# A message sum moved from a stage of its own into the mixer and the first feed-forward, and weight splitting moved out of the experts' stage into the mixer

## The chip, the cores and the metric

One NeuronCore of a Trainium2 chip runs the whole program in one launch. The metric is device microseconds of that core, lower is better. Before the change the three runs took 3969.18, 3976.69 and 3976.80 us; the median is 3976.69 us.

## What is computed

Two layers of a graph network on 3125 nodes with 256 channels and 50000 edges sorted by destination. The change touches the first layer alone, whose first half is (cut from the reference):

```python
# graph part, xn = layernorm(x)
h = xn @ W
norm = deg_inv_sqrt[src] * deg_inv_sqrt[dst]
out = segment_sum(h[src] * norm[:, None], dst, num_segments=N)
# mixer part, on the same xn
h = layernorm(x, ln1_g, ln1_b); xm = h @ Wx + bx
q = softmax(xm @ Wq, axis=-1); k = softmax(xm @ Wk, axis=-2); v = xm @ Wv
attn = (q @ (k.T @ v)) @ Wo + bo            # per head
fx = attn + x
m = gelu(layernorm(fx, ln2_g, ln2_b) @ W1 + b1) @ W2 + b2
# joined
x = x + out + (m + fx)
```

Then come eight experts (three 256x256 products each, weighted and added to `x`), and the second layer, whose last stage uses eight more experts with weights `L1_ffn_W1p` and `L1_ffn_W2p`. The graph sum and the mixer both depend only on `xn`, and both are added to `x`.

## The kernel before, in words

Rows lie in SBUF as 25 tiles of 125 nodes (`m.x`, `m.y`, `m.z`); most loops run over 5 chunks of 5 tiles. Products in float32 quality are made of float16 halves: an operand is scaled, its high half is copied by ScalarE and its low half is the rest, computed by VectorE. Each stage is a `phase` with its own tensors, semaphores and a barrier at its end, so stages don't overlap. Every engine runs its own instruction list in order, written by hand, and waits on semaphores.

The stages around the change, in order:

- **`message_sum`** (L646 to L711). The edges are 80 groups of 625. GpSimd issues 5 indirect DMAs per group (L657), each gathering 125 rows of 1 KB from DRAM into one of 4 slots. VectorE copies the indices of a group three ahead (L690), builds a one-hot matrix per group and tile that the group touches (L679), and adds the finished sum into `m.x` (L616, in class `Adder`). TensorE multiplies the one-hot by the gathered rows, 10 matmuls per visit (L708). A group has one visit or two; there are 104 visits. `total` has 4 PSUM banks (`RING`) and the adder runs 2 visits behind (`LAG`).
- **`layernorm_cols`** "ln1", then **`mixer0`** (L933 to L1117). The mixer has a first loop of 5 chunks (L979 to L1000: `mixed`, keys, queries and values), a middle part (softmax of the keys, their product with the values, L1003 to L1099) and a read loop of 5 chunks (L1102 to L1117). GpSimd adds two bias rows to `m.z` and `m.x` (L952).
- **`layernorm`** "ln2", then **`feed_forward`** "ff0": per chunk 16 units of 6 matmuls (L517 by helper `product`), Gelu on ScalarE (L861), two VectorE halves (L886, L888), then 5 row tiles of 24 matmuls (L840) that VectorE adds to `m.x` (L893).
- **`experts0`**: 8 experts times 5 chunks ("steps"). Beside its own work it prepares weights for the last stage: SyncE loads 2 MB of raw weights per expert (L1263, L1266), ScalarE makes the high half of a fifth in each step (L1355), VectorE the low half (L1406), and SyncE stores the halves (L1272). ScalarE and VectorE meet these instructions in order between those of the experts:

```python
act.wait_ge(s_raw, (e + 1) * 32)                                   # ScalarE, end of each step
act.activation(next16[:, 0, piece], next_raw[:, piece], ACT.Copy, scale=WS)
...
dve.wait_ge(s_nhigh, step + 1)                                     # VectorE, after the first row tile
dve.scalar_tensor_tensor(out=next16[:, 1, piece], in0=next_raw[:, piece], ...)
```

Of the kernel before, what the change touches and what calls it, by code (L numbers as in the profile page):

```python
# [15 lines left out]
F32 = mybir.dt.float32  # L16
# [13 lines left out]
J = 5  # L30
# [330 lines left out]
def layernorm(nc, m, name, source, rows_out=None, rows16=None):  # L361

    with phase(nc, name) as ph:
# [19 lines left out]
        with nc.Block() as block:  # L383

# [50 lines left out]
def layernorm_cols(nc, m, name, source, rows_out, cols):  # L435


    with phase(nc, name) as ph:
# [6 lines left out]
        s_normed, s_turned, s_free, s_done, s_rows = (ph.sem(x) for x in ("normed", "turned", "free", "done", "rows"))  # L445
        with nc.Block() as block:

            @block.vector
            def _(dve):
                v = Chain(dve, s_v)  # L450
                with dve.Fori(0, CHUNKS) as c:
                    for j in range(J):
                        ins = dve.bn_stats(stats[:, c * J + j, :], source[:, c * J + j, :])
                    ins.then_inc(s_stats, 1)
# [12 lines left out]
            @block.gpsimd  # L467
            def _(pool):
                if rows_out is not None:
                    with pool.Fori(0, CHUNKS) as c:  # L470
                        for j in range(J):
                            pool.wait_ge(s_normed, c * J + (j + 1))
                            pool.tensor_copy(rows_out[:, c * J + j, :], normed[:, j, :]).then_inc(s_rows, 1)

            @block.scalar
            def _(act):
# [3 lines left out]
                with act.Fori(0, CHUNKS) as c:  # L480
                    for j in range(J):
# [13 lines left out]
                        if rows_out is not None:  # L495
                            act.wait_ge(s_rows, c * J + (j + 1))
# [93 lines left out]
class Adder:  # L590
# [3 lines left out]
    def __init__(self, nc, dve, name, summed, total, s_total, s_added, scale=None):  # L594
        self.scale = scale
        self.nc, self.dve, self.summed, self.total = nc, dve, summed, total
        self.s_total, self.s_added = s_total, s_added
        self.tiles = [dve.alloc_register(f"{name}_tile{n}") for n in range(LAG)]
        for register in self.tiles:
            dve.reg_mov(register, 0)  # L600

    def add(self, visit, tile):
# [4 lines left out]
        fresh = self.total[:, dve.snap((visit + (RING - LAG)) % RING), 0:self.summed.shape[2]]  # L607
        for n in range(LAG - 1):
# [3 lines left out]
        dve.wait_ge(self.s_added, visit + LAG)  # L612
# [6 lines left out]
    def finish(self, visits, s_pace):  # L619

        for n in range(LAG):
            self.add(visits + n, 0)
        self.dve.wait_ge(self.s_added, visits + 2 * LAG)
# [3 lines left out]
def message_sum(nc, m, a):  # L627
# [4 lines left out]


    with phase(nc, "ms") as ph:
        index = ph.sb("index", [R, SLOTS, J], I32)
        got = ph.sb("got", [R, SLOTS, J, 2 * C], F16)
        hot = ph.sb("hot", [R, RING, J, R], F16)
        node = ph.sb("node", [R, T])
        s_node = ph.sem("node")
        total = ph.ps("total", [R, RING, 512])  # L640
        s_index, s_got = ph.sem("index"), [ph.sem(f"got{s}") for s in range(SLOTS)]
        s_hot, s_total, s_added, s_zero = (ph.sem(x) for x in ("hot", "total", "added", "zero"))
        s_pace = ph.sem("pace")
        ph.ahead(*[s_total, s_added] * LAG)

        with nc.Block() as block:  # L646

            @block.gpsimd
            def _(pool):
                pool.iota(node[:, :], pattern=[[R, T]], base=0, channel_multiplier=0,  # L650
                          allow_small_or_imprecise_dtypes=True).then_inc(s_node, 1)
                with pool.Fori(0, G // SLOTS) as i:
                    for s in range(SLOTS):
                        pool.wait_ge(s_index, i * SLOTS + (s + 1))
                        pool.sem_inc(s_pace, 1)
                        for j in range(J):
                            pool.indirect_dma_start(  # L657
                                out=got[:, s, j, :], out_offset=None, in_=m.gather0,
                                in_offset=bass.IndirectOffsetOnAxis(ap=index[:, s, j:j + 1], axis=0)
                            ).then_inc(s_got[s], 16)  # L660

            @block.vector
            def _(dve):
                dve.memset(total[:, :, :], 0.0).then_inc(s_zero, 1)
                dve.wait_ge(s_zero, 1)
                dve.wait_ge(s_node, 1)
                for s in range(SLOTS - 1):
                    dve.tensor_copy(index[:, s, :], m.edge_src[:, s, :]).then_inc(s_index, 1)
                adder = Adder(nc, dve, "ms", m.x, total, s_total, s_added, m.inv_sqrt_degree)

                with dve.Fori(0, G // SLOTS) as i:
                    for s in range(SLOTS):
                        g = i * SLOTS + s
                        first, count, before = group_bounds(dve, m, g)
                        with dve.Fori(0, count) as k:
                            visit = dve.snap(before + k)
                            tile = dve.snap(nc.s_assert_within(first + k, 0, T - 1))

                            dve.scalar_tensor_tensor(out=hot[:, visit % RING, :, :],  # L679
# [2185 lines left out]
```

## Time and profile before

| | us |
|---|---|
| median of three runs | 3976.69 |
| the profiled execution's own time | 3971.04 |
| its span, first to last instruction | 3969.2 |
| TensorE busy | 2597.7 (65%) |
| VectorE busy | 2161.6 (54%) |
| ScalarE busy | 1267.9 (32%) |
| GpSimd busy | 1311.2 (33%) |

The mean granted TensorE clock is 0.797 of full speed. The kernel is a sequence of stages, so a share of the whole span says little; each stage has to be read from its own stretch. "issue" in front of an instruction is time in which its engine waited for nothing that the profile shows, such as reading a register from memory.

### The profile page before, as it was taken

To read this page: it belongs to the slowest core of one execution; us is meant where nothing else is said; L and a number is where in the kernel's file an instruction comes from. 1 tells how busy PE (TensorE), PEld (TensorE's weight loads), DVE (VectorE), ACT (ScalarE), POOL (GpSimd) and SP (SyncE) were. 2 spreads that over 40 slices of the span, in tenths; PEclk is the share of its full clock that TensorE was granted. 3 is DMA by queue.
4 is the path that set the end of the run, shared out by engine and by line. 5 is a ranking of instruction groups with operands and counts; after the bars stand their busy time and mean duration, and the time that the engine had idled before them with its cause. 6 is when DMAs were issued, how large, how long until landed. Compare 5 with 4: busy or idle time off the path is not lost. (4 is left out here: it accounts for less than half of the span.)

```text
span 3969.2 us, 66443 instructions
## 1 busy us (share of the span) xinstructions
PE 2597.7 (65%) x17122; PEld 2094.4 (53%) x17123; DVE 2161.6 (54%) x4413; ACT 1267.9 (32%) x2476; POOL 1311.2 (33%) x1017
## 2 busy tenths in 40 slices
PE   5513333336587698896567777764967543699997
PEld 4413333334267466665455555543855442589986
DVE  6512222231556387787467777765533777644445
ACT  0300000003144154554122222223335774344541
POOL 0048888853000000000188888883000110211115
PEclk9655555557678599997789999996978875699998
DMA  3223333320000112211377777770000000356643
GB/s 110 72 66 84 83 84 83 83 64 6 0 22 0 37 51 100 100 50 71 99 194 189 190 190 191 187 181 28 0 14 0 0 0 0 147 190 237 233 147 90
DMA packets 240037, 364.49 MB, mean 92 GB/s; under 512 B 118099, under 2 KB 173728, under 8 KB 234588
## 3 DMA queue, kind: packets, MB, share of 16 engines
q0 software_dynamic: 154752, 174.53, 17.9%
q1 hardware_dynamic: 72348, 177.00, 12.9%
q10 hardware_dynamic: 12864, 12.06, 1.0%
q8 instruction: 37, 0.61, 0.1%
q14 instruction: 36, 0.29, 0.0%
HBM read 314.79 MB, written 47.76 MB: 91 GB/s over the span
## 5 line engine op out<-in xcount | busy, mean ns | idle before, releaser
L657 POOL DMA_INDIRECT ms_got<-gather,ms_index x400 | 497.6, 1244 | 125.1 <-issue 110.0
L708 PE MATMUL ms_total<-ms_got,ms_hot 125*125 125x256 f16 x1040 | 234.1, 414 | 411.8 <-DMA ms_got<-gather,ms_index 269.5
L1562 POOL DMA_INDIRECT as_gkv<-gather_kv,as_index x340 | 463.7, 1364 | 105.7 <-issue 101.4
L708 PEld LDWEIGHTS ms_total<-ms_got,ms_hot 125*125 x1040 | 205.6, 221 | 440.3 <-issue 440.3
L1554 POOL IOTA as_node<- 125x25 f32 x1 | 0.2, 156 | 1020.7 <-POOLq L116 1020.7
L1679 PE MATMUL as_total<-as_gkv,as_hot 125*125 125x264 f32 x850 | 217.9, 405 | 77.4 <-DVE as_summed L614 70.4
L1342 ACT ACTIVATE ex_h<-ex_up,ex_now 128x313 f32<-128x313 f32 (+1 forms) x320 | 193.7, 612 | 185.6 <-PE ex_up L517 179.7
L1679 PEld LDWEIGHTS as_total<-as_gkv,as_hot 125*125 125x125 f32 x850 | 157.0, 193 | 117.0 <-issue 91.4
L478 ACT ACTIVATE ln_sd<-ln_mv,eps 125x25 f32<-125x25 f32 x1 | 0.3, 317 | 681.0 <-DVEq L73 681.0
L2675 DVE CAST moe_hidden<-moe_h 128x256 f16<-128x256 f32 (+1 forms) x336 | 102.2, 304 | 199.7 <-ACT moe_h L2612 199.6
L2612 ACT ACTIVATE moe_h<-moe_up,wring 128x256 f32<-128x256 f32 (+1 forms) x336 | 163.5, 487 | 128.2 <-PE moe_up L517 85.8
L1654 PE MATMUL as_picked<-y_rows,as_pick 125*125 x1060 | 152.5, 294 | 47.8 <-issue 46.4
L2565 PE MATMUL moe_down<-wring,moe_hidden 128*128 128x256 f16 x1536 | 178.1, 273 | 0.0
L517 PE MATMUL ex_up<-ex_h,ex_w 128*128 128x313 f16 (+1 forms) x960 | 150.6, 318 | 42.0 <-DVE ex_h L1390 42.0
L517 PE MATMUL moe_up<-moe_cols,wring 128*128 128x256 f16 x1536 | 172.9, 273 | 1.4 <-ACT moe_cols L2619 1.4
L1654 PEld LDWEIGHTS as_picked<-y_rows,as_pick 125*125 x1060 | 125.5, 143 | 82.9 <-issue 80.0
L679 DVE SCALAR_TENSOR_TENSOR ms_hot<-row_no,ms_node,edge_dst 125x625 f32 x104 | 90.8, 873 | 134.0 <-issue 134.0
L2453 POOL DMA_INDIRECT moe_rows<-gather,moe_taken x64 | 63.2, 988 | 300.3 <-PE moe_turned L2540 257.7
L1390 DVE TENSOR_TENSOR ex_h<-ex_h 128x313 f16<-128x313 f32 (+1 forms) x320 | 155.4, 486 | 11.0
L517 PEld LDWEIGHTS moe_up<-moe_cols,wring 128*128 128x128 f16 x1536 | 150.2, 98 | 19.0 <-issue 1.6
L616 DVE SCALAR_TENSOR_TENSOR x_rows<-ms_total,inv_sqrt_degree,x_rows x106 | 50.9, 480 | 200.5 <-PE ms_total L708 199.6
L2565 PEld LDWEIGHTS moe_down<-wring,moe_hidden 128*128 128x128 f16 x1536 | 150.4, 98 | 17.3
(454 smaller groups left out, 6045.2 us busy)
## 6 DMA issues: line engine op xcount, KB each, us to landing
wring<-wsplit SPq DMA_DIRECT2D x33, 2052.0 KB
as_dsts<-in_dst SPq DMA_DIRECT2D x83, 305.2 KB
wsplit<-ex_next SPq DMA_DIRECT2D x8, 2048.0 KB, 8.7
ex_next_raw<-in_L_ffn_W1p SPq DMA_DIRECT2D x8, 1024.0 KB, 10.7
ex_next_raw<-in_L_ffn_W2p SPq DMA_DIRECT2D x8, 1024.0 KB, 12.9
results<-moe_made SPq DMA_DIRECT2D x32, 256.0 KB, 7.5
ms_got<-gather,ms_index POOLq DMA_INDIRECT x400
gather_kv<-qkv_out SPq DMA_DIRECT2D x5, 1250.0 KB
```

Of the source, the lines that this page charges most:

```text
L517: ins = pe.matmul(out, left(k, b), right(n, b), start=(i == 0), stop=(i == len(todo) - 1))
L657: pool.indirect_dma_start(out=got[:, s, j, :], out_offset=None, in_=m.gather0, in_offset=bass.IndirectOffsetOnAxis(ap=index[:, s, j:j + 1] ...
L679: dve.scalar_tensor_tensor(out=hot[:, visit % RING, :, :], in0=repeat_mid(m.row_no[0:R, :], J), scalar=node[:, bass.ds(tile, 1)], in1=repe ...
L708: ins = pe.matmul(total[:, visit % RING, 0:C], hot[:, visit % RING, j, :], got[:, s, j, p * C:(p + 1) * C], start=(j + p == 0), stop=(j + ...
L1342: act.activation(h32[:, u % 4, 0:n], up[:, u % 4, 0:n], ACT.Relu, bias=now[:, 1, layer, o:o + 1], scale=now[:, 0, layer, o:o + 1]).then_in ...
L1390: dve.tensor_tensor(to[:, 1, o, at:at + n], full, to[:, 0, o, at:at + n], ALU.subtract).then_inc(s_h, 1)
L1562: pool.indirect_dma_start(out=gkv[s][:, j, 0:2 * C], out_offset=None, in_=m.gather_kv, in_offset=bass.IndirectOffsetOnAxis(ap=index[:, s, ...
L1654: ins = pe.matmul(picked[:, j // 2, at:at + C], pick[:, visit % PICKS, j * R:(j + 1) * R], q16[:, tile, p, :], start=False, stop=False)
L1679: ins = pe.matmul(total[:, visit % RING, 0:W], hot[:, s, j, :], gkv[s][:, j, C:C + W], start=(j == 0), stop=(j == J - 1))
L2565: ins = pe.matmul(down[:, h, 0:C], hidden[:, k, f, h * 128:(h + 1) * 128], part(s, r, 1, f, 0, C), start=False, stop=(f == FB - 1 and n == 2))
L2612: act.activation(h32[:, u % 4, 0:n], up[:, u % 4, 0:n], ACT.Gelu, scale=1.0 / WS, bias=bias(s, f)).then_inc(s_h32, 1)
L2675: dve.tensor_copy(hidden[:, 0, f, at:at + n], full).then_inc(s_hhigh, 1)
```

## The change

The stage `message_sum` is gone. Its parts became the class `MessageSum`, whose tensors live over four stages, ln1 to ff0, and whose methods are called from those stages' instruction lists:

- `start` (VectorE) and the first 3 groups' gathers (GpSimd) run in ln1; VectorE also adds the bias row `L0_mix_b2` to all of `m.x` there, which GpSimd did in the mixer.
- 40 groups are dealt over the mixer, 4 in each chunk of the first loop and 4 in each chunk of the read loop; none in the middle part. 40 groups are dealt over ff0, 8 per chunk: one after every fourth unit and one after each of the first four row tiles. The gathers of the first 3 of these are issued in ln2.
- PSUM is shared now: `total` has 2 banks and the adder runs 1 visit behind; the mixer's bank of 4 became 2, and so did ff0's `down`.

`Splitter` takes the weight splitting out of `experts0` into the mixer: 16 half-steps, each with two loads, two ScalarE copies, two VectorE instructions and two stores of 128x1024 values, 10 half-steps in the first loop and 6 in the first three chunks of the read loop. In the mixer the bias of `m.z` moves from GpSimd to VectorE as well.

```diff
+class Splitter:
+    def move(self, sp, e, h):
+        i = e * 2 + h
+        for s in range(2):
+            sp.wait_ge(self.s_whole[s], i + AHEAD)
...
+            sp.dma_start(to, taken).then_inc(self.s_raw[s], 16)
...
+        for s in range(2):
+            sp.wait_ge(self.s_whole[s], i + 1 + AHEAD)
+            sp.dma_start(...).then_inc(self.s_stored[s], 16)
+    def high(self, act, i):
+        for s in range(2):
+            act.wait_ge(self.s_raw[s], (i + 1) * 16)
+            act.wait_ge(self.s_stored[s], i * 16 + AHEAD)
+            act.activation(self.split[:, s, 0, :], self.raw[:, s, :], ACT.Copy, scale=WS).then_inc(self.s_half[s], 1)
+    def low(self, dve, i):
+        for s in range(2):
+            dve.wait_ge(self.s_half[s], i + 1)
+            dve.scalar_tensor_tensor(out=self.split[:, s, 1, :], in0=self.raw[:, s, :], scalar=WS,
+                                     in1=self.split[:, s, 0, :], op0=ALU.mult, op1=ALU.subtract)\
+                .then_inc(self.s_whole[s], 1)
+class MessageSum:
+    def gather(self, pool, trip, slots=range(SLOTS)):
+        for s in slots:
+            pool.wait_ge(self.s_index, trip * SLOTS + (s + 1))
+            for j in range(J):
+                pool.indirect_dma_start(...).then_inc(self.s_got[s], 16)
+    def spread(self, dve, trip, s):
+        g = trip * SLOTS + s
+        first, count, before = group_bounds(dve, self.m, g)
+        with dve.Fori(0, count) as k:
...
+            dve.scalar_tensor_tensor(out=self.hot[:, visit % RING, :, :], ...).then_inc(self.s_hot, 1)
+            self.adder.add(visit, tile)
+        free = (s - 1) % SLOTS
+        dve.wait_ge(self.s_total, before + 1)
+        dve.wait_ge(self.s_added, before + count + 1)
+        dve.tensor_copy(self.index[:, free, :], nxt).then_inc(self.s_index, 1)
+    def products(self, pe, trip, s):
+        first, count, before = group_bounds(pe, self.m, g)
+        pe.wait_ge(self.s_got[s], (trip + 1) * (16 * J))
+        with pe.Fori(0, count) as k:
+            pe.wait_ge(self.s_hot, visit + 1)
+            pe.wait_ge(self.s_added, visit + 1)
...
 def layernorm_cols(nc, m, name, source, cols, ms, bias):
+                ms.start(dve)
+                dve.tensor_tensor(m.x[:, :, :], m.x[:, :, :], repeat_mid(bias, T), ALU.add)
...
+                ms.number(pool)
+                ms.gather(pool, 0, range(SLOTS - 1))
 def mixer0(nc, m, a, ms):                      # first loop
+                    for s in (0, 1):
+                        ms.products(pe, c, s)
...
+                        if j == 1:
+                            ms.products(pe, c, 2)
+                    ms.products(pe, c, 3)
...
+                    for h in range(2):
+                        splitter.high(act, c * 2 + h)
...
+                    for s in (0, 1):
+                        ms.spread(dve, c, s)
+                    some = m.z[:, bass.ds(c * J, J), :]
+                    dve.tensor_tensor(some, some, repeat_mid(bo, J), ALU.add).then_inc(s_bias, 1)
...
+                        if j == 1:
+                            ms.spread(dve, c, 2)
+                            splitter.low(dve, c * 2)
+                    ms.spread(dve, c, 3)
+                    splitter.low(dve, c * 2 + 1)
 def feed_forward(...):
+                        if ms is not None and u % 4 == 3:
+                            ms.products(pe, c * 2 + trip, u // 4)
...
+                        if ms is not None and j < SLOTS:
+                            ms.products(pe, c * 2 + (trip + 1), j)
...
+                        if ms is not None and u % 4 == 1:
+                            dve.wait_ge(s_added, c * J + AHEAD)
+                            ms.spread(dve, c * 2 + trip, u // 4)
 def experts0(nc, m, a):
-                            act.wait_ge(s_raw, (e + 1) * 32)
-                            act.wait_ge(s_stored, e * 16 + AHEAD)
-                            act.activation(next16[:, 0, piece], next_raw[:, piece], ACT.Copy, scale=WS)\
-                                .then_inc(s_nhigh, 1)
...
-                                    dve.wait_ge(s_nhigh, step + 1)
-                                    dve.scalar_tensor_tensor(out=next16[:, 1, piece], in0=next_raw[:, piece], ...)
```

Before, VectorE's list in the first loop of the mixer holds two copies per tile and nothing else (`mix_q` and `y_rows` take query and value out of PSUM):

```order
L1066 ISA
L1066 COPY mix_q<-mix_rbank 125x32
L1067 ISA
L1067 COPY y_rows<-mix_rbank 125x256
L1065 REGISTER_ALU
```

Now the same place, between the second tile's copies and the third's, reads (`ms_hot` is the one-hot, `x_rows` the adder's target, `mix_split` the weight halves):

```order
L1167 COPY y_rows<-mix_rbank 125x256
L585 ISA
L585 TENSOR_LOAD group_table
...
L737 SCALAR_TENSOR_TENSOR ms_hot<-row_no,ms_node,edge_dst 125x625
...
L618 SCALAR_TENSOR_TENSOR x_rows<-ms_total,inv_sqrt_degree,x_rows 125x256
...
L749 ISA
L749 COPY ms_index<-edge_src 125x5
L680 ISA
L682 SCALAR_TENSOR_TENSOR mix_split<-mix_raw,mix_split 128x1024 x2
```

A register load, the one-hot, the adder with its wait for TensorE, the index copy and two splitting instructions now stand in front of the third tile's copies, and TensorE waits for those copies before it may reuse `mix_rbank`.

TensorE's list in ff0 before, units of 6 matmuls back to back:

```order
L517 MATMUL ff_up<-z_flat,ff_w 128x313 x6
L517 MATMUL ff_up<-z_flat,ff_w 128x312 x6
```

And now, after the fourth unit:

```order
L519 MATMUL ff_up<-z_flat,ff_w 128x313 x6
L519 MATMUL ff_up<-z_flat,ff_w 128x312 x6
L585 ISA
L585 TENSOR_LOAD group_table
...
L760 UNCONDITIONAL_BRANCH
...
L766 MATMUL ms_total<-ms_got,ms_hot 125x256 x2
...
L760 COMPARE_AND_BRANCH
L895 REGISTER_ALU
```

The group's products, with their waits for the gather and for the one-hot, stand between the fourth unit and the fifth; the Gelu and halves of the fifth can't start before them.

## Rows read from the trace of the kernel before

**Rows 1.** The page: span of the profiled execution.
```profile
span 3969.2 us, 66443 instructions
```

**Rows 2.** Windows, stage by stage: us, busy by engine, PEclk, DMA share, GB/s.
```profile
244.00:875.70 631.70, 234.09 (x1040) 205.59 (x1040) 157.53 (x294) 0.00 (x0) 497.77 (x401) 0.54 0.34 82
875.70:917.00 41.30, 15.90 (x50) 7.59 (x50) 19.99 (x58) 20.44 (x51) 0.00 (x0) 0.50 0.00 0
917.00:1078.80 161.80, 109.48 (x376) 63.01 (x376) 50.31 (x117) 26.70 (x47) 30.19 (x15) 0.76 0.01 4
1078.80:1112.20 33.40, 11.40 (x100) 10.11 (x100) 27.30 (x83) 21.68 (x52) 0.00 (x0) 0.50 0.00 0
1112.20:1262.70 150.50, 138.48 (x1112) 119.84 (x1112) 76.70 (x190) 52.54 (x89) 0.00 (x0) 0.93 0.04 14
1365.90:1854.70 488.80, 427.28 (x3120) 316.20 (x3120) 379.84 (x932) 244.03 (x420) 0.00 (x0) 0.93 0.23 83
```

**Rows 3.** Groups of instructions in the message sum, 244 to 876 us.
```profile
L657 POOL DMA_INDIRECT ms_got<-gather,ms_index x400 | 497.6, 1244 | 125.1 <-issue 110.0 <-DVE ms_index L690 11.9 <-DVE ms_index L668 3.3
L708 PE MATMUL ms_total<-ms_got,ms_hot 125*125 125x256 f16 x1040 | 234.1, 414 | 411.8 <-DMA ms_got<-gather,ms_index 269.5 <-DVE ms_hot L679 102.7 <-DVE x_rows L616 39.6
```

**Rows 4.** Timeline of the message sum: start, us, engine, line [idle before <-releaser].
```profile
254.15 1.21 POOL L657 DMA_INDIRECT ms_got<-gather,ms_index  x1 [0.30 <-issue]
...
259.28 2.36 PE L708 MATMUL ms_total<-ms_got,ms_hot 125*125 125x256 f16 x10 [31.54 <-DMA ms_got<-gather,ms_index]
...
263.53 0.87 DVE L679 SCALAR_TENSOR_TENSOR ms_hot<-row_no,ms_node,edge_dst 125x625 f32 x1 [1.44 <-issue]
264.32 0.48 DVE L616 SCALAR_TENSOR_TENSOR x_rows<-ms_total,inv_sqrt_degree,x_rows  x1
...
266.90 2.36 PE L708 MATMUL ms_total<-ms_got,ms_hot 125*125 125x256 f16 x10 [5.26 <-DMA ms_got<-gather,ms_index]
```

**Rows 5.** Windows of the mixer: first loop, middle part, read loop; last, ff0's loop.
```profile
931.30:995.70 64.40, 60.37 (x220) 37.31 (x220) 13.65 (x50) 14.67 (x30) 16.88 (x6) 0.97 0.00 0
995.70:1029.20 33.50, 18.45 (x81) 9.73 (x81) 13.00 (x23) 11.71 (x16) 0.00 (x0) 0.87 0.00 0
1029.20:1077.60 48.40, 30.66 (x75) 15.95 (x75) 23.66 (x45) 0.00 (x0) 0.00 (x0) 0.50 0.00 0
1129.50:1261.60 132.10, 131.49 (x1080) 112.94 (x1080) 71.77 (x185) 47.96 (x85) 0.00 (x0) 0.99 0.00 0
```

**Rows 6.** Groups of instructions in the mixer and in ff0 that serve as prices.
```profile
L1117 DVE TENSOR_TENSOR x_rows<-x_rows,y_rows x5 | 7.5, 1491 | 0.6
L871 DVE SCALAR_TENSOR_TENSOR ff_w<-ff_w,ff_gain_s 128x1024 f16<-128x1024 f32 x2 | 2.5, 1280 | 11.8 <-ACT ff_w L852 11.8
```

**Rows 7.** The second layer's attention sum: its gathers as a group, then one collision.
```profile
L1562 POOL DMA_INDIRECT as_gkv<-gather_kv,as_index x305 | 418.9, 1374 | 94.8 <-issue 90.8 <-DVE as_index L1709 4.0
...
2321.73 1.49 DVE L1703 TENSOR_TENSOR z_flat<-z_flat 125x1280 f32<-125x1280 f32 x1
...
2321.91 2.38 POOL L1562 DMA_INDIRECT as_gkv<-gather_kv,as_index  x1 [0.30 <-issue]
```

**Rows 8.** Windows: a stretch of the attention sum, and one of the first router.
```profile
1300.00:1350.00 50.00, 35.12 (x198) 27.32 (x197) 11.15 (x25) 0.57 (x2) 0.00 (x0) 0.50 0.00 0
2100.00:2150.00 50.00, 35.29 (x196) 26.97 (x196) 37.93 (x47) 14.51 (x23) 41.02 (x30) 1.00 0.76 191
```

**Rows 9.** Experts' stage: two groups of ScalarE, one step's length, the last load.
```profile
L1355 ACT ACTIVATE ex_next<-ex_next_raw x40 | 35.1, 878 | 46.6 <-DMA ex_next_raw<-in_L_ffn_W2p 46.6
L1349 ACT ACTIVATE ex_w<-ex_w x40 | 18.0, 451 | 0.0
...
1534.95 0.45 ACT L1349 ACTIVATE ex_w<-ex_w  x1
...
1545.28 0.45 ACT L1349 ACTIVATE ex_w<-ex_w  x1
...
ex_next_raw<-in_L_ffn_W2p SPq DMA_DIRECT2D x8, 1024.0 KB, 12.9
```

More of the change, by code:

```diff
@@ L383, in layernorm, with _ @@
         with nc.Block() as block:
+            @block.gpsimd
+            def _(pool):
+                if ms is not None:
+                    ms.gather(pool, trip, range(SLOTS - 1))
             @block.vector
@@ L606, in add @@
         into = self.summed[:, oldest, :]
[L607 to L608 removed]
+        fresh = self.total[:, dve.snap((visit + (self.ring - self.lag)) % self.ring), 0:self.summed.shape[2]]
+        for n in range(self.lag - 1):
             dve.reg_mov(self.tiles[n], self.tiles[n + 1])
@@ L807, in feed_forward, with _ @@
         with nc.Block() as block:
+            @block.gpsimd
+            def _(pool):
+                if ms is not None:
+                    ms.gather(pool, trip, range(SLOTS - 1, SLOTS))
+                    with pool.Fori(1, 2 * CHUNKS) as t:
+                        ms.gather(pool, trip + t)
             @block.sync
@@ L929, in mixer0 @@
         s_act, s_bias, s_added = ph.sem("act"), ph.sem("bias"), ph.sem("added")
-        bo, b2 = m.row["L0_mix_bo"], m.row["L0_mix_b2"]
+        bo = m.row["L0_mix_bo"]
+        splitter = Splitter(nc, m, a, ph)
+        LATE = X8 - CHUNKS
         nbd = 3 * X8
@@ L947, in _ @@
                     .then_inc(s_mask, 1)
-                with pool.Fori(0, CHUNKS) as c:
-                    for rows, bias in ((m.z, bo), (m.x, b2)):
-                        some = rows[:, bass.ds(c * J, J), :]
-                        ins = pool.tensor_tensor(some, some, repeat_mid(bias, J), ALU.add)
-                    ins.then_inc(s_bias, 1)
+                ms.gather(pool, 0, range(SLOTS - 1, SLOTS))
+                with pool.Fori(1, 2 * CHUNKS) as t:
+                    ms.gather(pool, t)
             @block.sync
@@ L965, in _ @@
                     sp.dma_start(wqv[p, h // 4, at:at + HD], a["L0_mix_Wv"]).then_inc(s_bd, 16)
+                with sp.Fori(0, X8) as e:
+                    for h in range(2):
+                        splitter.move(sp, e, h)
+                splitter.finish(sp)
             @block.tensor
@@ L1050, in _ @@
                             .then_inc(s_kout, 1)
+                    for h in range(2):
+                        splitter.high(act, c * 2 + h)
                 act.wait_ge(s_kmax, 1)
@@ L1057, in _ @@
                 act.activation(q[:, :, :], q[:, :, :], ACT.Exp).then_inc(s_qexp, 1)
+                with act.Fori(CHUNKS, X8) as e:
+                    for h in range(2):
+                        splitter.high(act, e * 2 + h)
             @block.vector
@@ L1117, in _ @@
                     dve.tensor_tensor(x, x, y, ALU.add).then_inc(s_added, 1)
+                    dve.wait_ge(s_added, c + 1)
+                    ms.spread(dve, c + CHUNKS, 3)
+                    if splits:
+                        splitter.low(dve, (c + CHUNKS) * 2 + 1)
+                with dve.Fori(0, LATE) as c:
+                    read_chunk(c, True)
+                with dve.Fori(LATE, CHUNKS) as c:
+                    read_chunk(c, False)
 def router(nc, m, name, Wr, br, bias2):
```

276 lines of the change are left out of this document (131 added, 145 removed).

## The prediction

> **What bounds the kernel now.** I read the windows by stage first, then the groups and the timeline of the message sum, then the mixer, ff0 and the experts.
>
> The span is 3969.2 us [rows 1]; the execution's own time is 3971.04 and the median 3976.69, so I sum against 3971 and move the result up by 6. The five stages that the change merges take 631.7 + 41.3 + 161.8 + 33.4 + 150.5 = 1018.7 us [rows 2]. The message sum has 498 us of GpSimd in its 632, and only 234 of TensorE and 158 of VectorE. It is bound by the issue of gathers: 400 at 1.244 us with 0.31 between them [rows 3], 7.8 us for a group of five. The longest wait of its products is for a landing gather. In the four other stages GpSimd issues no gather at all. So one side has a free GpSimd and the other a nearly free TensorE and VectorE: the merged stages can't be shorter than the gathers (some 620 us), and can't be better than that by any other overlap.
>
> The experts' stage takes 488.8 us [rows 2]. A step is 1545.28 - 1534.95 = 10.33 us, 40 steps are 413. ScalarE waited 46.6 us, 7 times, for the raw weights of the other layer, and never for the stage's own weights [rows 9].
>
> **ln1.** 41.3 us, plus the bias on 25 tiles: 5 x 1.49 = 7.5 [rows 6], plus some 2 for clearing two banks and the indices. **51 us.** The 15 gathers there need 15 x 1.55 = 23 us and are hidden; they start while the bias is added.
>
> **The mixer's first loop.** A chunk takes 64.4 / 5 = 12.9 us, 12.1 of them TensorE at a clock of 0.97 [rows 5]. Now TensorE has gaps. Of its clock the rows speak two ways: 35 us of 50 busy went with 0.50 in the router, and the same 35 with 1.00 in the attention sum [rows 8]. I take 0.65 between them, which makes the chunk's own matmuls 18 us. Then come 4 groups. A visit of 10 matmuls took 2.36 us at the low level [rows 4], and there are 1.3 visits per group, 3.1 us: 12.3 for four. The one-hots of the third and fourth group stand directly in front of their products, each with a register read of 1.44 and 0.87 for itself [rows 4]: 4.6. The first two are made early, but TensorE reads the group's register too; no row shows it apart, so between 0 and VectorE's 1.44 I take the latter, the nearest row: 2.9 for two. Copies and semaphores add 1, ScalarE some 2 (below). Sum **41 us per chunk, 205 for five** (GpSimd alone would need 4 x 8.1 = 32, all hidden). In front stand the 14.3 us of weight loading, from 917.0 to 931.3.
>
> **The splitter.** A half-step needs 2 MB moved between two `low` calls, two ScalarE copies and two VectorE instructions of 1.28 us [rows 6]. The experts' loads land 12.9 us after issue, behind 3.75 MB more [rows 9]: 2 MB need at least 12.9 x 2 / 4.75 = 5.4 us. From above: the attention sum moved 191 GB/s in all [rows 8] and the gathers take 82 [rows 2], which leaves 109, so 19 us. I take 10, nearer the experts' row, since theirs is the same transfer. ScalarE holds the next chunk's `mixed` behind the second `high`; from the first `low` to the next chunk TensorE and VectorE have about 10 us of work, so 2 us of it show.
>
> **Middle part.** 33.5 us [rows 5], with no group in it. GpSimd runs out of indices after three groups, 24 us. Add 4.5 for the last half-step in front of it: **38 us**.
>
> **Read loop.** Here VectorE's list is the chain. Its own work is 23.66 / 5 = 4.7 us per chunk [rows 5]. A group costs it 1.44 + 0.87 + 0.48 + 0.4 for the index copy, and 0.8 for its share of second visits: 4.0, times four is 16. Two half-steps are 5.1. Waits for products that stand between row tiles add some 5.5. That is 31.3 in three chunks and 26.2 in two: 146; with edges **152 us**. GpSimd needs 17 x 8.1 = 138 in it. The mixer is 14 + 205 + 38 + 152 = **409 us** against 161.8.
>
> **ln2** stays at 33.4: the 15 gathers fit under it.
>
> **ff0.** GpSimd is the bound here. A gather is slower beside busy VectorE: 1.374 us in the attention sum against 1.244 [rows 3, 7], and one that started 0.18 us into a 1.49 us VectorE instruction took 2.38 [rows 7]. With 0.31 between them a group costs 7.8 by the one row and 8.4 by the other; I take 8.1. The first gather comes 17.3 us after the start (1112.2 to 1129.5) plus 3 for the first `spread`; 37 groups are 300; landing (255.4 to 259.3 is 3.9 [rows 4]), last product, last row tile and add are 10. The chain of the in-order lists is near it: between two products stand 2 units, their Gelu and halves, and the next one-hot, 7 to 10 us by the clock. For that I add 8. **338 us** against 150.5. TensorE's 26.4 us per chunk [rows 5] are hidden; without that cover they cost nothing until 60 us per chunk.
>
> The collision above says that a gather waits for such a VectorE instruction to end. The Trainium skill (SBUF — State Buffer, "Who interferes with whom") reports a probe in which a `tensor_copy` stalled a DMA issued from GpSimd "but `tensor_tensor` and `tensor_reduce` not". By that, one-hots and subtractions would not slow a gather: 1.21 + 0.31 each, 7.6 us a group, and ff0 19 us shorter. This trace disagrees with it.
>
> **Experts.** 488.8 - 413 leaves 76 us. Some 15 are the first weights and the end of the stage; 60 belong to the 7 changes of expert, of which 46.6 are the wait and the rest a lower clock behind it. With the loads gone all of it goes; the own weights land in time already. The 0.88 and 1.0 us per step of ScalarE and VectorE are hidden by TensorE and give nothing. **60 us gained**, 47 to 65.
>
> **Sum.** 51 + 409 + 33 + 338 = 831, which is 187 less than 1018.7; with 60 it is 247. 3971 - 247 = 3724, as a median **3730 us**. A measurement of this kernel tells some 0.2% (8 us) from nothing.
>
> **Rivals.**
>
> *A: gathers bound everything* (16%). If the mixer's chains hide under GpSimd, it is 22 + 37 x 8.1 + 15 idle in the middle = 337, and ff0 is 326 or a little more: 84 less, **3646**. For it: the attention sum keeps GpSimd 41 of 50 us busy with TensorE at 35 and VectorE at 38 [rows 8]. Against it: its lists are made for that, the mixer's chunk has three turns between engines.
>
> *B: TensorE at the low level in ff0 and the mixer* (13%). Then an ff0 chunk is 2 x 26.4 + 10.4 x 2.36 + 8 x 1.44 = 89 us, over GpSimd's 65, 5 chunks and 20 are 465 instead of 338, and the mixer gains another 20: **3877**. The router's row speaks for it, the attention's against.
>
> *C: the splitter's trip* (8%). 19 us instead of 10 beside the gathers, on ScalarE and VectorE in order, adds 9 or so in 8 chunks: **3800**.
>
> *D: slower* (5%). The place is the index copy at the end of `spread`: it is queued behind VectorE's waits for products. If VectorE falls more than three groups (23 us) behind, GpSimd stops, the next product waits for issue and landing, and this repeats in each chunk. With all overlap lost the merged stages are 1018.7 again, plus entry to each group (1.44 + 1.44 + 0.87) x 80 = 300, less the 60 of the experts: **4210**. It decides from 3.1 us more per group than my sum has (247 / 80). Against it: the attention sum holds its pace with the same lead.
>
> *E: the experts' wait only changes its name* (3%), from the other layer's weights to the own ones. Then 187 are left: **3790**. The own-weight row with 0.0 of idle speaks against.
>
> **Numbers.** My forecast has 55%. The range reaches from A to just short of B, 3645 to 3860, which leaves out most of B, D and the far ends. Faster than before by over 0.2%: 94%; within it: 1%; slower: 5%.
>
> **What would show it.** Right: gathers issued from ln1 on, with GpSimd's idle time in the mixer's middle part; a first-loop chunk near 41 us and a read chunk near 30; ff0 near 338 with gathers of 1.25 to 1.37 us back to back and TensorE's longest wait on `ms_got`; experts near 429 with no ScalarE wait on a DMA. Wrong: TensorE over 90% busy in ff0 at a clock near 0.5 (B); ScalarE waiting on `mix_raw` (C); GpSimd idle in ff0 with `ms_index` as releaser (D); an idle time in front of the experts' own weight copies (E).

## The result, and the profile after

The change takes 3688.76 us (median of four runs, 3687.74 to 3690.03) against 3973.18 for the kernel before beside it: a ratio of 0.9285, with a 95% interval of 0.9268 to 0.9301. It is faster by 284 us. The forecast was 3730 us and 247 us gained: the direction and the range held, the gain was sized 37 us too small. The measured time lies midway between the forecast and rival A (3646), so the total alone can't tell the two apart; the stages and the experiments have to.

The page's span, which answers to [rows 1]:

```profile
span 3686.0 us, 66570 instructions
```

The windows stage by stage (us, busy time of each engine, PEclk, DMA share, GB/s), as in [rows 2]: ln1, mixer, ln2, ff0, experts.

```profile
243.50:294.40 50.90, 15.91 (x50) 7.61 (x50) 29.47 (x63) 20.35 (x51) 23.86 (x16) 0.50 0.16 38
294.40:670.90 376.50, 218.67 (x896) 155.96 (x896) 172.68 (x301) 58.90 (x79) 244.68 (x188) 0.71 0.60 154
670.90:705.10 34.20, 11.40 (x100) 10.11 (x100) 28.34 (x83) 21.59 (x52) 18.77 (x15) 0.50 0.24 57
705.10:1044.30 339.20, 232.54 (x1632) 197.71 (x1632) 160.71 (x335) 52.22 (x89) 241.48 (x185) 0.88 0.31 77
1147.10:1573.60 426.50, 413.81 (x3120) 309.45 (x3120) 355.68 (x892) 215.33 (x380) 0.00 (x0) 0.98 0.05 17
```

| stage | before | forecast | after |
|---|---|---|---|
| message sum | 631.7 | gone | gone |
| ln1 | 41.3 | 51 | 50.9 |
| mixer | 161.8 | 409 | 376.5 |
| ln2 | 33.4 | 33.4 | 34.2 |
| ff0 | 150.5 | 338 | 339.2 |
| experts | 488.8 | 429 | 426.5 |

The five merged stages gave 1018.7 - 800.8 = 218 us and the experts 62; the spans differ by 283, so 3 us came from elsewhere. Only the mixer is clearly off, by 32 us. Its windows are the first loop, the middle part and the read loop, as in [rows 5]:

```profile
309.00:483.70 174.70, 111.49 (x480) 78.44 (x480) 80.26 (x143) 34.34 (x50) 124.36 (x94) 0.85 0.70 184
483.70:517.80 34.10, 18.98 (x81) 9.80 (x81) 13.02 (x24) 13.60 (x18) 1.21 (x1) 0.80 0.20 58
517.80:670.00 152.20, 88.20 (x335) 67.72 (x335) 76.24 (x129) 10.57 (x10) 111.86 (x85) 0.54 0.58 148
```

The first loop took 35 us per chunk, not 41; the read loop 152, as forecast. Now the groups that answer to [rows 3]: the products of the first loop, those of the read loop, then the gathers and products of ff0.

```profile
L766 PE MATMUL ms_total<-ms_got,ms_hot 125*125 125x256 f16 x260 | 43.8, 332 | 48.9 <-DVE ms_hot L737 47.6 <-DVE x_rows L618 1.3
...
L766 PE MATMUL ms_total<-ms_got,ms_hot 125*125 125x256 f16 x260 | 59.6, 419 | 58.7 <-DVE ms_hot L737 41.3 <-DMA ms_got<-gather,ms_index 9.7 <-DVE x_rows L618 4.6
...
L714 POOL DMA_INDIRECT ms_got<-gather,ms_index x185 | 241.5, 1305 | 94.6 <-issue 49.8 <-DVE ms_index L749 44.8
L766 PE MATMUL ms_total<-ms_got,ms_hot 125*125 125x256 f16 x520 | 78.7, 308 | 91.8 <-DVE ms_hot L737 67.8 <-DMA ms_got<-gather,ms_index 21.3 <-issue 1.5
```

Before, TensorE waited longest for a landing gather. Now it waits for the one-hot everywhere: the wait for data has become a wait for VectorE's list. That holds in ff0 too, where the prediction expected the longest wait to be for a gather: 67.8 us for the one-hot against 21.3. GpSimd has two long waits: this one, from the gathers of ln2 to the first group of ff0, and one of 36.88 us in the mixer's middle part.

```profile
731.48 1.21 POOL L714 DMA_INDIRECT ms_got<-gather,ms_index  x1 [36.80 <-DVE ms_index L749]
```

In the experts, ScalarE's wait of [rows 9] for the other layer's weights is gone with its copies; the own weights still wait for nothing.

```profile
L1444 ACT ACTIVATE ex_w<-ex_w x40 | 18.0, 449 | 0.0
```

### The profile page after: what moved, and what is told of

The parts are those of the page before. It is cut to its first block and busy times, and to the rows that moved or that the text cites. A ratio compares the mean times of both kernels' runs of the same rounds, so it can differ in the third digit from the quotient of the medians.

```text
span 3686.0 us, 66570 instructions
## 1 busy us (share of the span) xinstructions
PE 2557.8 (69%) x17122; PEld 2056.4 (56%) x17123; DVE 2198.5 (60%) x4412; ACT 1270.5 (34%) x2468; POOL 1303.7 (35%) x1005
## 5 line engine op out<-in xcount | busy, mean ns | idle before, releaser
L714 POOL DMA_INDIRECT ms_got<-gather,ms_index x400 | 527.4, 1319 | 235.3 <-issue 119.4
L766 PE MATMUL ms_total<-ms_got,ms_hot 125*125 125x256 f16 x1040 | 182.2, 342 | 199.4 <-DVE ms_hot L737 156.7
L766 PEld LDWEIGHTS ms_total<-ms_got,ms_hot 125*125 x1040 | 154.5, 175 | 231.9 <-issue 231.7
L930 ACT ACTIVATE ff_h<-ff_up,ff_bias 128x313 f32<-128x313 f32 (+1 forms) x160 | 83.5, 522 | 281.5 <-PE ff_up L519 260.2
L1818 DVE SCALAR_TENSOR_TENSOR as_hot<-row_no,as_node,edge_dst 125x625 f32<-125x625 f32 x104 | 90.6, 871 | 125.7 <-PE as_total L1762 78.1
L2760 DVE TENSOR_TENSOR moe_hidden<-moe_h,moe_hidden 128x256 f16<-128x256 f32 (+1 forms) x336 | 148.3, 441 | 11.5
```

The source lines that it names most:

```text
L714: pool.indirect_dma_start(out=self.got[:, s, j, :], out_offset=None, in_=self.m.gather0, in_offset=bass.IndirectOffsetOnAxis(ap=self.index ...
L766: ins = pe.matmul(self.total[:, visit % 2, 0:C], self.hot[:, visit % RING, j, :], self.got[:, s, j, p * C:(p + 1) * C], start=(j + p == 0) ...
L2760: dve.tensor_tensor(hidden[:, 1, f, at:at + n], full, hidden[:, 0, f, at:at + n], ALU.subtract).then_inc(s_hidden, 1)
```

## The experiments

Edits are shown cut. Lines in plain words inside them tell what is moved and are not code.

### The splitting back in the experts, the message sum dealt out

```diff
-        splitter = Splitter(nc, m, a, ph)          # mixer0: and its move, high and low calls
+        experts0: load_next, store_next and the two pieces per step, as before the change
```

> The change with one part undone: the weight splitting is back in the experts' stage as before, the message sum stays dealt out. My theory: the experts' stage goes back to 488.8 us (+62), and the mixer loses what the splitter shows there, by the prediction's terms 2 us in each first-loop chunk, 4.5 in the middle part and 5.1 in three read chunks, 30 us in all: mixer 376 to 346, total 3689 + 62 - 30 = 3721 us. Rival 1, the splitter is hidden in the mixer: mixer 376, total 3751. Rival 2, the splitter's trips set the mixer's pace: the mixer falls by 60 or more, total 3690 or less, and moving the splitting was worth nothing.

Measured 3727.1 us (ratio to before 0.9383, 0.9367 to 0.9399), 38 more than the change. Windows: first loop, middle, read loop, experts.

```profile
310.40:463.80 153.40, 110.13 (x473) 77.55 (x474) 56.88 (x123) 14.67 (x30) 109.18 (x86) 0.86 0.29 71
463.80:497.30 33.50, 19.30 (x90) 10.36 (x88) 13.03 (x24) 11.71 (x16) 11.45 (x10) 0.82 0.16 42
497.30:646.60 149.30, 83.12 (x335) 64.63 (x335) 62.54 (x117) 0.33 (x1) 108.63 (x85) 0.58 0.30 74
1124.00:1612.00 488.00, 425.68 (x3120) 315.47 (x3120) 379.62 (x932) 243.99 (x420) 0.00 (x0) 0.94 0.23 83
```

The experts are back at 488. The mixer lost 21.3 us in the first loop, 0.6 in the middle and 2.9 in the read loop. So the two halves of the change separate: some 62 us from the experts, and the splitter costs 25 where it went: 4.3 per first-loop chunk (2 were forecast) and 1 per read chunk with a splitter (5.1 were). What it costs in the first loop can be read in the change's own trace, in VectorE's low halves and ScalarE's high halves there:

```profile
L682 DVE SCALAR_TENSOR_TENSOR mix_split<-mix_raw,mix_split 128x1024 f16<-128x1024 f32 x20 | 24.1, 1225 | 22.7 <-ACT mix_split L676 22.4
L676 ACT ACTIVATE mix_split<-mix_raw 128x1024 f16<-128x1024 f32 x20 | 20.7, 1050 | 90.5 <-DMA mix_raw<-in_L_ffn_W1p 74.7 <-DMA mix_raw<-in_L_ffn_W2p 15.8
```

The two half-steps of a chunk don't stand evenly: the second low half began 12 to 13 us after the first, and the next chunk's 21 to 24 us after that. At the short distance VectorE stood and waited for ScalarE, which waited for the load, 22.4 us in all.

### The splitter moved alone, the message sum left as a stage

```diff
 (kernel before)
+    mixer0: splitter.high / low / move at the same places as in the change
-    experts0: its splitting
```

> The kernel before with only the splitter moved into its mixer and out of the experts; the message sum stays a stage of its own. My theory: the experts gain 62 us here too, but the mixer (161.8 us) has no cover for 16 half-steps: each needs its transfers between two low halves, 5 to 10 us, so a first-loop chunk goes from 12.9 to some 18, the middle waits 5, and three read chunks go from 9.7 to some 20: mixer 225, total 3973 - 62 + 63 = 3974, no change. Rival, the transfers and halves fit beside the mixer's own work: mixer 180, total 3930. If the gain of the experts does not appear without the rest of the change, it is 3990 or more.

Measured 3981.21 us, ratio 1.0019 (1.0005 to 1.0032): 7.5 us slower than before, where no change was forecast. First loop and read loop:

```profile
930.90:1037.30 106.40, 71.89 (x220) 43.13 (x220) 41.74 (x71) 33.78 (x50) 17.00 (x6) 0.82 0.61 187
1071.30:1145.20 73.90, 31.29 (x75) 16.44 (x75) 37.57 (x57) 10.87 (x11) 0.00 (x0) 0.50 0.50 156
```

Against 64.4 and 48.4 [rows 5] the splitter costs 42 and 25.5 us here; with the gathers beside it, it cost 21 and 3. The experts' gain is worth taking here only because the message sum stretches the mixer and covers the rest.

### Three gathers of five

The run leaves out 2 of the 5 gathers of each group (the products read the first three again).

```diff
-            for j in range(J):
+            for j in range(3):
                 pool.indirect_dma_start(out=self.got[:, s, j, :], ...)
-        pe.wait_ge(self.s_got[s], (trip + 1) * (16 * J))
+        pe.wait_ge(self.s_got[s], (trip + 1) * (16 * 3))
```

> The change with 3 of the 5 gathers of each group left out of account (two are not made; the products read the first three again), so GpSimd's work per group falls from 8.1 to 4.9 us, and nothing else changes. My theory: ff0 is bound by the issue of gathers with the chain of in-order lists close behind (7 to 8 us per group): ff0 falls from 339 to 290 to 310. The mixer's loops are bound by the in-order lists: the first loop stays at 175 us (within 5) and the read loop at 150 (within 8). Rival A, gathers bound everything: the first loop falls to 130 or less and ff0 to 220. Rival chain: ff0 stays within 5 us of 339, its lists bind it and the gathers were hidden.

Measured 3633.09 us (0.9145, 0.9126 to 0.9163). First loop, read loop, ff0:

```profile
307.90:475.20 167.30, 112.79 (x480) 80.62 (x480) 80.01 (x143) 34.58 (x50) 75.46 (x57) 0.85 0.59 164
509.30:654.70 145.40, 84.63 (x335) 64.03 (x335) 75.37 (x130) 10.92 (x11) 67.33 (x51) 0.56 0.47 125
688.40:978.60 290.20, 217.39 (x1632) 184.01 (x1632) 156.38 (x335) 52.24 (x89) 142.18 (x111) 0.92 0.23 57
```

The two loops moved by 7.4 and 6.8 us, while GpSimd's work in them fell by some 49 and 45: they are bound by the in-order lists in the main, though the first loop moved by more than the 5 expected. ff0 fell by 49.0, though its gathers became 40% fewer: over 37 groups that is 1.3 us each, from 8.1 to 6.8, where the lists take over. ff0 is bound by gathers, but with little room. The change's trace says the same: GpSimd waited 1.27 and 0.89 us for an index in front of the second and third group of ff0, and never more than 0.31 after that.

### The high halves of ff0 on ScalarE

```diff
+    act.activation(hidden[:, 0, f, at:at + n], h32[:, u % 4, 0:n], ACT.Copy).then_inc(s_hhigh, 1)
-    dve.tensor_copy(hidden[:, 0, f, at:at + n], full).then_inc(s_hhigh, 1)
```

> The change with the high half of the feed-forward's hidden values (160 copies of 128x313, 0.434 us each on VectorE in ff0) made by ScalarE instead; ScalarE has 52 us of work in 339 there. My theory: a gather that meets a VectorE instruction waits for it, so 69 us less of VectorE work makes the gathers of ff0 shorter, 1.30 to about 1.26 us, 7 us in ff0, total 3682. Rival chain: the way from Gelu to the low half gets longer by 0.2 to 0.4 us per unit and the gathers do not matter: ff0 the same or some us longer, total 3690 to 3700, gathers perhaps shorter all the same. Rival, two-input instructions alone disturb a gather: the gathers keep their mean.

Measured 3685.05 us (0.9269, 0.9248 to 0.9291), which can't be told from the change. The stage shows it: ff0 took 332.9 us against 339.2, and its gathers

```profile
L714 POOL DMA_INDIRECT ms_got<-gather,ms_index x185 | 234.2, 1266 | 95.4 <-issue 51.3 <-DVE ms_index L749 44.1
```

fell from 1305 to 1266 ns, 7.3 us in all. Taking VectorE work away shortens gathers by what was expected.

### Extra matmuls in the read loop

```diff
+    def warm():
+        for n in range(4):
+            pe.matmul(kbank[:, 0, 0:C], wk[:, n % 2, :], wo[:, n % 2, :], start=True, stop=True)
+    warm()                       # in front of each ms.products of the read loop
```

> The change with four extra matmuls (32x256, float32, into a bank that is free) in front of each group's products in the mixer's read loop, 80 in all, where the granted clock is 0.5 to 0.59 and a visit's ten products take 2.39 us instead of 1.30. If the clock follows what TensorE does, it rises towards 1.0 there and the visits fall to 1.3 us: 26 visits x 1.09 = 28 us gained against 1 to 2 us for each set of extra matmuls, 20 to 40 us, where they are not hidden in TensorE's waits; the read loop stays within 15 us of 150. Rival, the clock does not rise: visits stay at 2.4 us and the loop grows by 20 to 40 us.

Measured 3694.55 us (0.929, 0.9269 to 0.9311); the read loop's window, then the group of its products:

```profile
518.40:668.30 149.90, 110.06 (x495) 64.88 (x495) 75.53 (x129) 10.90 (x11) 111.09 (x85) 0.81 0.59 150
```

```profile
L766 PE MATMUL ms_total<-ms_got,ms_hot 125*125 125x256 f16 x260 | 40.0, 312 | 31.6 <-DMA ms_got<-gather,ms_index 12.3 <-DVE ms_hot L737 12.3 <-issue 6.4
```

The extra matmuls are 49.0 us of TensorE work. With them the granted clock rose from 0.54 to 0.81 and the 26 visits fell from 59.6 to 40.0 us, so TensorE was busy 22 us more in all. The loop gained 2 us: the extra work was hidden in TensorE's waits, and the visits it made faster were mostly hidden too. No gain in total: it is 6 us slower than the change, with overlapping intervals.

### Groups moved to where GpSimd is idle

```diff
 mixer0, middle part, behind the c-th product of keys and values (c = 0 to 3):
+    ms.products(pe, CHUNKS, c)          # TensorE
+    ms.spread(dve, CHUNKS, c)           # VectorE, in front of its wait for that product
 feed_forward: no groups beside the row tiles of chunk 0
```

> The change with 4 groups moved from ff0 (the row tiles of its first chunk) into the mixer's middle part, where GpSimd stood idle for 36.9 us; each is put behind one of the first four products of keys and values. My theory: ff0 is bound by gathers and falls by 4 x 8.1 = 32 us; the middle part (34 us, a chain of turns of 3.85 us each, VectorE waiting 2.5 of them) takes a group for 3 to 4 us of TensorE, +14. Total 3689 - 32 + 14 = 3671 us. Rival: GpSimd's idle time only moves, since the groups of the middle part wait for their own gathers (8.1 each): the middle grows by 30, total 3687, no gain.

Measured 3681.68 us (0.9256, 0.924 to 0.9271), 7 less than the change with intervals that just overlap. Middle part and ff0:

```profile
486.60:528.70 42.10, 27.63 (x131) 16.23 (x131) 20.30 (x38) 13.62 (x18) 26.40 (x22) 0.78 0.42 109
716.70:1035.20 318.50, 223.54 (x1582) 189.38 (x1582) 149.72 (x321) 47.00 (x85) 214.15 (x165) 0.88 0.30 74
```

A group in the middle part cost 2 us, not 3.5. But ff0 gave back 5.2 us per group, not 8.1: behind the bared row tiles GpSimd waited 12.84 us for an index (to 789.33 us); behind the first group of ff0 its longest wait in the change is 1.27. All four groups were taken from one chunk, and the lists are the bound there for a while. The next run moves 4 more into ln2, and bares the second chunk of ff0 as well.

> As the run before, and 4 more groups moved from ff0 (the row tiles of its second chunk) into ln2, one behind each of its first four chunks. ln2's VectorE is busy for 28 of 34 us, so a group costs it some 3.5 us: ln2 +14, ff0 another -32 (GpSimd's wait at the start of ff0, 36.8 us, is used). Total 3653 us. Rival: ln2's second visits and its waits for gathers cost 8 us per group, which leaves nothing: 3671.

Measured 3687.13 us (0.9273, 0.9257 to 0.9288), no gain over the change. The profiled execution was the fastest of four (3677.57; the others took 3685.74 to 3688.68), so its stages show more gain than the median has. ln2 took 60.7 us instead of 34.2: 6.6 us per group, near the rival's 8. ff0 took 291.3. What a group costs in a list that has no slack is what it costs in ff0.

### The splitter in ff0

```diff
 mixer0: no splitter
 feed_forward, chunks 0 to 3:
+    for n in range(4):                       # ScalarE, after the last unit
+        splitter.high(act, c * 4 + n)
+    if j < 4:                                # VectorE, after row tile j
+        splitter.low(dve, c * 4 + j)
```

> The change with the weight splitting in ff0 instead of the mixer: four half-steps in the row-tile part of each of its first four chunks, in the room of its own raw weights. My theory: the mixer falls by the 24 us that it fell without the splitter, and in ff0, bound by gathers, ScalarE and VectorE have room; only the 32 two-input instructions of 1.23 us make some gathers wait, up to 1 us each: +10 us (0 to 25). Total 3675 us. Rival: ff0's chain of lists (7.2 us per group in the run with three gathers) is so near that 2.5 us per half-step comes on top: ff0 +35, total 3700.

Measured 3724.97 us (0.9364, 0.9347 to 0.9381). The mixer fell as in the first run, but ff0 grew from 339.2 to 394.8, far above the forecast and even the rival. ScalarE's group in ff0:

```profile
L676 ACT ACTIVATE ff_w<-ff_w 128x1024 f16<-128x1024 f32 x32 | 33.3, 1054 | 164.6 <-DMA ff_w<-in_L_ffn_W1p 144.9 <-DMA ff_w<-in_L_ffn_W2p 19.7
```

and the way from one low half to the next in the timeline of VectorE and ScalarE, 14.1 us, where row tiles come every 8:

```profile
747.56 1.23 DVE L682 SCALAR_TENSOR_TENSOR ff_w<-ff_w 128x1024 f16<-128x1024 f32 x1 [7.93 <-ACT ff_w L676]
...
752.59 0.36 SPq L659 DMA_DIRECT2D ff_w<-in_L_ffn_W1p  x1
...
760.46 1.06 ACT L676 ACTIVATE ff_w<-ff_w 128x1024 f16<-128x1024 f32 x1 [10.32 <-DMA ff_w<-in_L_ffn_W1p]
...
761.66 1.22 DVE L682 SCALAR_TENSOR_TENSOR ff_w<-ff_w 128x1024 f16<-128x1024 f32 x1 [6.83 <-ACT ff_w L676]
```

That is the mechanism of the prediction's rival C, in full: the half-step's trip (store, load, high half, low half) sets the pace. So it was spaced out:

```diff
-    four half-steps beside row tiles 0 to 3
+    after units 7 and 15, and after row tiles 1 and 3
```

> The weight splitting in ff0 as in the run before it, but its four half-steps per chunk spaced out: after the 8th and 16th unit and after the 2nd and 4th row tile, some 16 us apart instead of 8. That run was 60 us longer in ff0, and its trace has 14.1 us from one low half to the next (747.56 to 761.66 us), with ScalarE waiting for the load. My theory: that trip set the pace there; at 16 us apart it fits, and what is left is the collisions of 32 two-input instructions with gathers: ff0 339 + 10 (0 to 25), mixer 24 less, total 3675 us. Rival, the work itself is too much for the lists (3.5 us per half-step): total 3720 again, wherever it stands in ff0.

Measured 3664.87 us (five runs, 3664.09 to 3667.32; ratio 0.9227, 0.9212 to 0.9242): **24 us faster than the change, with intervals apart.** Windows of the first loop, the read loop and ff0, then ScalarE's group in ff0:

```profile
309.70:461.90 152.20, 109.71 (x474) 76.93 (x475) 57.51 (x123) 14.65 (x30) 108.74 (x87) 0.87 0.30 72
495.40:644.80 149.40, 82.68 (x335) 64.35 (x335) 62.85 (x117) 0.33 (x1) 108.72 (x85) 0.59 0.30 74
678.50:1023.90 345.40, 237.63 (x1632) 200.74 (x1632) 194.08 (x367) 82.54 (x119) 248.16 (x185) 0.85 0.67 173
```

```profile
L676 ACT ACTIVATE ff_w<-ff_w 128x1024 f16<-128x1024 f32 x32 | 33.4, 1053 | 112.6 <-DMA ff_w<-in_L_ffn_W1p 88.0 <-DMA ff_w<-in_L_ffn_W2p 24.6
```

The same work in the same stage costs 6 us in place of 56. GpSimd's wait for an index in ff0 was 100.2 us in the dense run and is 46.1 here; VectorE's wait for the high halves fell from 68.9 to 22.5. The low halves now begin 12 to 25 us apart, so the trip still shows at the shortest distance, but no longer paces the stage.

### Three edits together, and one taken back

> Three edits together on the change: 4 groups in the mixer's middle part (-7 us when alone), the high half of the hidden values on ScalarE in ff0 (-4 alone, -6.5 in its ff0), and the splitting spaced out in ff0's last four chunks (-14 forecast). If they add up: 3689 - 25 = 3664 us. Rival: with the copies and the highs both on ScalarE its list becomes the chain of ff0, and 3680 or more comes out.

Measured 3692.08 us (0.9297, 0.928 to 0.9313): the gains do not appear, and ff0 took 360 us. To tell why, the copies went back to VectorE:

> The run with three edits together gave 3692 us where 3664 was forecast; its ff0 was 357 us where the parts added up to 314, with 95 us of GpSimd's idle time on an index. Here one of the three is taken back: the high half of the hidden values is made by VectorE again. 4 groups stay in the mixer's middle part, the splitting stays spaced out in ff0's last four chunks. My theory: on ScalarE a copy stood behind two splitting copies and their waits for loads, and the low half behind the copy, so that ScalarE's list became the chain; without it the other two add up: 3665 - 12 (by stages: +6 in the middle, -21 in ff0, of which some 5 are lost to the chain) = 3653 us, ff0 321 us. Rival: splitting in four chunks instead of in the first four of five, beside an uncovered first chunk, is what cost it; then it is 3680 or more again.

Measured 3693.89 us (0.93, 0.9287 to 0.9313), ff0 362.4: my theory of ScalarE's list fell. The rival's number came (3680 or more), but the trace of this last run shows another cause for most of it. VectorE at the turn of its loop in ff0 (start, us), with nothing that holds it:

```profile
892.83 0.42 DVE L1005 SCALAR_TENSOR_TENSOR x_rows<-ff_down,x_rows 125x256 f32 x1
903.71 0.33 DVE L990 CAST ff_hidden<-ff_h 128x313 f16<-128x313 f32 x1 [10.46 <-issue]
```

It does so at each of the three turns, 9.51, 10.46 and 10.14 us, 30 of the 41 us by which ff0 missed its 321, if all of it shows. The run with all three edits has the same gaps, 10.17, 8.97 and 9.85 us. The other 11 us stay open. The queues of the DMA in the gap from 893.3 to 903.7 (packets, MB, share) hold a kind that is seldom seen:

```profile
q1 hardware_dynamic: 1007, 1.69, 55.7%
q0 software_dynamic: 747, 0.76, 40.4%
q14 instruction: 2, 0.02, 1.2%
```

Over the whole of ff0 this instruction queue brought 21 packets, and 7 in the spaced run, which has no such gap. Each of the six gaps of the two runs holds exactly 2 of them. So code was being fetched while data held the DMA engines for 96% of the time; that the gap is the wait for this code is inferred, not tried. The Trainium skill (Advanced Engine Details and Errata, "ISA Cache") gives an engine's sequencer two lines of 256 instructions; by that, a loop that touches a third would be fetched anew each turn. The trace agrees as far as it goes: packets at every turn. Why nearly the same loop body brings them in one program and not in the other was not tried. In the spaced run the loop is chunks 0 to 3 with the last chunk's code behind it, in these two it is chunks 1 to 4 with the first chunk's in front; that its place in memory decides is only a guess.

### What holds up a gather

The last kernel leaves out the bias `L0_mix_b2`.

```diff
-    dve.tensor_tensor(m.x[:, :, :], m.x[:, :, :], repeat_mid(bias, T), ALU.add)
+    dve.tensor_scalar(m.x[:, :, :], m.x[:, :, :], 1.0, None, ALU.mult)
```

> The change with ln1's bias added to x left out; in its place a one-input multiplication by 1.0 of the same 125x6400 values, to see what a gather beside it does. In the change the two-input addition took 6.83 us and the gather that began 1.3 us into it took 6.56 instead of 1.21. If any VectorE instruction on SBUF holds a gather up until its end, the gather beside this one lasts as long as the instruction (3.4 us if it runs at twice the rate). If only two-input instructions do, it takes 1.2 us. The total changes by 0 to -4 us.

One execution, 3680.56 us. Its timeline in ln1, then the change's:

```profile
245.11 4.20 POOL L714 DMA_INDIRECT ms_got<-gather,ms_index  x1 [0.97 <-DVE ms_index L721]
245.47 3.50 DVE L457 TENSOR_SCALAR x_rows<-x_rows 125x6400 f32<-125x6400 f32 x1 [0.19 <-DVE ms_total L722]
248.88 7.28 DVE L460 BATCH_NORM_STATS2 ln_stats<-z_rows  x22
249.62 1.21 POOL L714 DMA_INDIRECT ms_got<-gather,ms_index  x1 [0.31 <-issue]
```

```profile
245.14 6.83 DVE L457 TENSOR_TENSOR x_rows<-x_rows,rowvec 125x6400 f32<-125x6400 f32 x1 [0.17 <-DVE ms_total L722]
246.48 6.56 POOL L714 DMA_INDIRECT ms_got<-gather,ms_index  x1 [0.31 <-issue]
```

Both instructions hold a gather until they are over, 4.20 and 6.56 us instead of 1.21; the gathers ended 0.3 and 1.1 us after them. The statistics do not (1.21 beside them). So the collision is not a matter of two inputs alone. The two cases differ in one thing: the one-input instruction held a gather that had begun 0.36 us before it, while the gather that began 0.35 us before the addition took 1.38 us and only the next one was held. Each rests on a single execution.

## Why the prediction was right, and where it was off

- **ln1, ln2, ff0, experts**: 50.9, 34.2, 339.2 and a gain of 62.3 us against 51, 33.4, 338 and 60. The experts' step is shown by undoing it; besides the 46.6 us of wait, TensorE's busy time there fell by 13.5 us at a clock of 0.98 instead of 0.93, as the "lower clock behind it" said. ff0's bound is shown by the run with three gathers. Its groups ran at 8.1 us as taken, but that the stage came out within 1 us is partly luck: the first gather came 26 us after the start, not 20, and 13.6 us stood behind the last one, not 10, while the 8 us that were added for the chain of the in-order lists did not show (GpSimd's waits for an index behind the first group come to under 2 us beyond the 0.3 in front of every gather).
- **The first loop** is the step that failed: 35 us per chunk, not 41. The mechanism was right and its size off. The TensorE clock was set at 0.65 "between" two rows and was 0.85. The chunk's own matmuls took (111.49 - 43.8) / 5 = 13.5 us, not 18, and a visit 43.8 / 26 = 1.68 us, not 2.36, which is 3.5 less for 5.2 visits. The splitter showed 4.3, not 2. 41 - 4.5 - 3.5 + 2.3 = 35.3, and 34.9 was measured. What this leaves for waits and entries, 13.0 us, is near TensorE's idle time of 12.6 per chunk, but its terms (4.6, 2.9, 1, 2) were not measured one by one. Its in-order lists bind it, as said.
- **The middle part** took 34.1, not 38: the 4.5 us for the last half-step in front of it did not show; GpSimd stood idle there as forecast.
- **The read loop** came out right (152.2) by luck, with a wrong split. The prediction made VectorE's list the chain and priced the splitter at 5.1 us per pair of half-steps on it. Without the splitter VectorE's busy time in the loop fell from 76.24 to 62.54 us and the loop by only 3, 1 us a pair: VectorE's list alone is not the chain. Relieving TensorE, the gathers or the splitter gave 2, 7 and 3 us; none alone is the chain. VectorE waited 38.8 us for products of TensorE there and TensorE 54.0 for VectorE, so presumably the turns between the two lists hold it; that was not taken apart.
- **Rivals.** A did not come: the mixer's lists bind, at 35 us per 4 groups where GpSimd needs 32. B did not: ff0 ran at 0.88. C came in a small way in the mixer: its sign, ScalarE waiting on `mix_raw`, is there with 90.5 us in the first loop, and at the 12 us between a chunk's two low halves the trip set VectorE's pace. That cost 21 us where 10 were priced, not the 72 more of C. It came in full when four half-steps stood in the row-tile part of ff0. D: GpSimd's waits for an index are 115 us, but 74 of them are the two gaps that were forecast. E did not.
- **The collision term** held: gathers of 1.305 us in ff0, between the 1.244 and 1.374 of the two rows, and the run with the copies on ScalarE moved it by the forecast amount. The probe that the Trainium skill reports (SBUF — State Buffer, "Who interferes with whom"), in which a `tensor_tensor` did not stall a DMA issued from GpSimd, was weighed in the prediction and does not carry over to these gathers: 6.56 us beside 6.83. The same section also says that an instruction with two SBUF inputs contends with a GpSimd instruction that reads SBUF. A gather takes its indices from SBUF, so this trace can agree with that; no run tells whether reading them is what waits.

## What to carry to other kernels

When work of one engine is dealt out over stages that leave that engine free, each stage then costs the larger of the dealt engine's time and its own in-order list, so price both per unit of work, and take the clock from what TensorE will be doing then. A side job with a load, a copy and a store has a trip time (12 to 14 us here); crowded into one part of the loop it set the pace and cost 56 us, spread over the whole loop it cost 6. A gain measured alone is not yet a gain together: edits worth 7 and 24 us gave none when joined, and most of what was missing were three stops of some 10 us that neither had alone.

## What the hardware showed that was not expected

- Code loads seem to wait in line with data: VectorE stood for some 10 us at each of three loop turns, with 2 packets of an instruction queue in the gap and, in the one shown, the DMA engines 96% taken by data. Two runs have it, and none took it apart.
- TensorE's granted clock rose with its own work: 49.0 us of extra matmuls in 150 us, 22 us more of busy time in all, raised it from 0.54 to 0.81 of full speed in the mean.
- A one-input `tensor_scalar` in SBUF holds up a gather's issue (4.20 us beside 3.50) as a two-input addition does (6.56 beside 6.83), and statistics don't (1.21); seen once each.
